# ScalarE's high copy of the first tile ahead of its copy of keys and queries, and two small changes in the tail, in a gated cross-attention and expert kernel

## What is computed

```python
# x (8,256,128), ctx (8,512,128), 16 heads of 64
xn   = layernorm(layernorm(x)) * gamma + beta
q, k, v = heads(xn @ w_q), *heads(split(ctx @ w_kv))
attn = softmax(q * 64**-0.5 @ k.T)
x    = x + tanh(g_xattn) * tanh(gate) * (merge(attn @ v) @ w_out + b_out)
# the expert layer's `combine` and `dispatch` follow from argmax and a cumulative count
p    = softmax(layernorm(x) @ gate_w)
slot = place of a token among those of its expert (dropped from 160 on)
y    = relu(expert_tokens @ w1[e]) @ w2[e]
out  = x + tanh(g_ffn) * p_max * y[slot]
```

## Time and profile before

| | |
|---|---|
| median of 3 runs | 475.69 us (475.61 to 476.74) |
| profiled execution | 475.53 us, of which the span of its instructions is 473.7 us |
| PE busy | 439.7 us, 93% |
| PEld busy | 334.0 us, 71% |
| ACT busy | 386.4 us, 82% |
| DVE busy | 360.3 us, 76% |
| POOL busy | 356.6 us, 75% |

### The profile page before, as it was taken

How to read it: one execution, slowest core, us unless ns; L and a number is a source line. 1 busy time by engine, 2 the same in 40 slices (tenths; PEclk the granted TensorE clock), 3 DMA queues, 4 the chain that set the end, 5 groups by cost and what they waited for, 6 DMA issues and landing times.

```text
span 473.7 us, 13155 instructions
## 1 busy us (share of the span) xinstructions
PE 439.7 (93%) x5096; PEld 334.0 (71%) x5096; DVE 360.3 (76%) x789; ACT 386.4 (82%) x630; POOL 356.6 (75%) x270
## 2 busy tenths in 40 slices
PE   7889799998999989999999999999999999988993
PEld 6656667776767767776777667776777677758892
DVE  4787687778877887779787796878877887785622
ACT  5889788899888988899888898899799998892330
POOL 3687686888788887888878877898878877871325
PEclk9999999999999999999999999999999999999998
DMA  5499999999999999999999999999989998996021
GB/s 167 150 177 192 206 187 175 170 181 204 188 176 188 210 194 180 192 192 192 198 189 197 189 196 191 185 200 209 190 157 185 193 180 147 159 182 137 14 67 46
DMA packets 283037, 82.10 MB, mean 173 GB/s; under 512 B 264387, under 2 KB 280435, under 8 KB 282976
## 3 DMA queue, kind: packets, MB, share of 16 engines
q1 hardware_dynamic: 281600, 77.96, 93.4%
q0 software_dynamic: 1376, 3.30, 2.2%
HBM read 10.83 MB, written 5.14 MB: 34 GB/s over the span
## 4 chain that ended last, share of the span: by engine, by line
PE 40%; DVE 20%; ACT 16%; DMA 10%; issue 8%; POOL 4%; POOLq 0%; SPq 0%; ACTq 0%; DVEq 0%
DVE MXL L903 9%; DMA PT<-PARTS 9%; ACT P L752 7%; DVE HL L890 4%; ACT HL L714 4%; PE psAB L1234 3%; PE psX L1319 3%; PE psAB L1241 3%; PE psO L1267 3%; ACT PARTS L762 3%; POOL PARTS L650 3%; PE psX L1355 3%; DVE VL L896 3%; PE psO L1269 3%; PE psO L1268 3%
## 5 line engine op out<-in xcount | busy, mean ns | idle before, releaser
L650 POOL TENSOR_TENSOR PARTS<-P,PARTS 128x1024 f16<-128x1024 f32 x125 | 267.4, 2145 | 63.5 <-ACT PARTS L762 61.8
L762 ACT ACTIVATE PARTS<-P 128x1024 f16<-128x1024 f32 x126 | 136.1, 1080 | 0.7
L752 ACT ACTIVATE P<-psAB,NB 128x512 f32<-128x512 f32 x128 | 81.6, 695 | 41.8 <-DVE NB L906 41.4
L903 DVE TENSOR_REDUCE MXL<-psAB 128x2 f32<-128x1024 f32 x64 | 78.4, 1224 | 41.4 <-PE psAB L1241 23.9
L1267 PE MATMUL psO<-VH,PT 128*128 128x65 f16 x1008 | 98.6, 194 | 8.3 <-DMA PT<-PARTS 7.7
L1267 PEld LDWEIGHTS psO<-VH,PT 128*128 128x128 f16 x1008 | 92.0, 98 | 12.0 <-DMA PT<-PARTS 8.9
L1268 PE MATMUL psO<-VL,PT 128*128 128x64 f16 x1008 | 98.5, 192 | 0.0
L1269 PE MATMUL psO<-VH,PT 128*128 128x65 f16 x1008 | 98.4, 193 | 0.0
L1268 PEld LDWEIGHTS psO<-VL,PT 128*128 128x128 f16 x1008 | 91.3, 98 | 0.5
L1269 PEld LDWEIGHTS psO<-VH,PT 128*128 128x128 f16 x1008 | 91.5, 97 | 0.0
L752 ACT ACTIVATE P<-psCD,NB 128x512 f32<-128x512 f32 x128 | 81.7, 703 | 0.1
(11 more groups left out here) (214 smaller groups left out, 871.7 us busy)
## 6 DMA issues: line engine op xcount, KB each, us to landing
ctx_raw<-in_ctx_dram SPq DMA_DIRECT2D x8, 256.0 KB, 3.7
w1s<-in_L_ffn_w_dram SPq DMA_DIRECT2D x8, 256.0 KB, 3.6
w2s<-in_L_ffn_w_dram SPq DMA_DIRECT2D x8, 256.0 KB, 4.0
PT<-PARTS SPq DMA_TRANSPOSE x126, 5.0
experts_table<-zeros POOLq DMA_DIRECT2D x2, 645.0 KB, 4.0
X<-in_x_dram SPq DMA_DIRECT2D x8, 128.0 KB, 4.2
wraw<-in_L_xattn_w_kv_dram SPq DMA_DIRECT2D x4, 256.0 KB, 5.3
out_dram<-row SPq DMA_DIRECT2D x8, 128.0 KB, 2.5
```

The source lines that it names most:

```text
L650: pool.tensor_tensor(PARTS[:, par, qt, 1], P32[:, par, qt], PARTS[:, par, qt, 0], ALU.subtract).then_inc(plo_done, 1)
L752: last = act.activation(P32[:, par, qt, SK * h:SK * h + SK], score_bank(qt)[:, SK * h:SK * h + SK], ACT.Exp, bias=NB[:, par, qt, h:h + 1])
L762: act.activation(PARTS[:, hp % 2, qt, 0], P32[:, hp % 2, qt], ACT.Copy).then_inc(phi_done[qt], 1)
L903: dve.tensor_reduce(MXL[:, par, qt, :, 0], score_bank(qt)[:].rearrange("p (h n) -> p h n", h=2), AX.X, ALU.max, negate=True).then_inc(max_ ...
```

## The change

In every step but the last, `phi(b, hp, 0)` moves from behind `kq_hi`, `v_hi` (hp 2), `xt_copy` (hp 4) and `tokt_copy` (hp 5) to a place right behind the exponentials of the first tile. In the tail, the values of pair 63 go to psAB instead of psO, with a third row of `rden`, and neither they nor the values of pair 62 wait for the division of the pair just ahead (63 waits for ScalarE to have read psAB, 62 for the division of 61). The output rows come in seven groups, (0,1) (2,3) (4) (5) (6) (7) (8,9), instead of five pairs; the last two groups stand behind the last `down`, and VectorE copies yT of the last two experts ahead of them.

```diff
@@ scalar engine, batch(b)
                     exps(b, hp, 0)
+                    if j < LAST:
+                        phi(b, hp, 0)
                     if not (is_last(b) and hp + AHEAD >= PAIRS):
                         kq_hi(*next_pair(b, hp, AHEAD))
...
                         tokt_copy(b - 1)
-                    if j < LAST:
-                        phi(b, hp, 0)
                     exps(b, hp, 1)
@@ values (tensor engine)
-                if j:
-                    pe.wait_ge(norm_done, turn(j) - 1)
+                sums = value_bank(j)
+                if j == LAST:
+                    pe.wait_ge(pthi_done, 1)
+                elif j:
+                    pe.wait_ge(norm_done, j)
...
-        OUT_GROUPS = ST_TILES // 2
-        ROWS_AFTER = [-(-2 * P * (i + 1) // CAP) - 1 for i in range(OUT_GROUPS)]
+        OUT_GROUPS = ((0, 1), (2, 3), (4,), (5,), (6,), (7,), (8, 9))
+        ROWS_AFTER = [-(-P * (tiles[-1] + 1) // CAP) - 1 for tiles in OUT_GROUPS]
...
+        def value_bank(j):
+
+            return psAB if j == LAST else psO
@@ after the experts (tensor engine)
             down(E - 1)
-            rows_out(OUT_GROUPS - 1)
+            for i, after in enumerate(ROWS_AFTER):
+                if after >= E - 2:
+                    rows_out(i)
```

More of the change, by code:

```diff
@@ L114, in gated_block @@
         NB = sb("NB", [P, 2, QT, 2], F32)
-        rden = sb("rden", [P, 2, 2 * QT], F32)
+        rden = sb("rden", [P, 3, 2 * QT], F32)
         O = sb("O", [P, QT, INNER], F32)
@@ L910, in normalise_heads @@
                 j = b * PAIRS + hp
-                sums = psO[:, 0:2 * QT * (DH + 1)].rearrange("p (g d) -> p g d", d=DH + 1)
+                sums = value_bank(j)[:, 0:2 * QT * (DH + 1)].rearrange("p (g d) -> p g d", d=DH + 1)
                 n = turn(j)
+                r = 2 if j == LAST else hp % 2
                 dve.wait_ge(pv_done, n)
-                dve.reciprocal(rden[:, hp % 2, :], sums[:, :, DH]).then_inc(rden_done, 1)
+                dve.reciprocal(rden[:, r, :], sums[:, :, DH]).then_inc(rden_done, 1)
                 dve.wait_ge(rden_done, n)
@@ L920, in normalise_heads @@
                 dve.tensor_tensor(o, sums[:, :, 0:DH].rearrange("p (h q) d -> p h q d", h=2),
-                                  rden[:, hp % 2, :].rearrange("p (h q) -> p h q", h=2).unsqueeze(3)
+                                  rden[:, r, :].rearrange("p (h q) -> p h q", h=2).unsqueeze(3)
                                   .to_broadcast([P, 2, QT, DH]), ALU.mult).then_inc(norm_done, 1)
@@ L1149, in y_rows @@
                 dve.wait_ge(yrow_psum, i + 1)
-                for n in range(2):
-                    t = 2 * i + n
+                for n, t in enumerate(OUT_GROUPS[i]):
                     dve.scalar_tensor_tensor(out=yrows[:, t, :], in0=FFN_BANKS[i % 2][:, P * n:P * n + P],
@@ L1158, in _ @@
                 dve.tensor_copy(yT[:, e * CAP:(e + 1) * CAP], [psO, psX][e % 2][:, 0:CAP]).then_inc(y_done, 1)
-                for i in range(OUT_GROUPS):
-                    if ROWS_AFTER[i] == e:
+                for i, after in enumerate(ROWS_AFTER):
+                    if after == e < E - 2 or after >= E - 2 and e == E - 1:
                         if i == 0:
@@ L1266, in values @@
                             first_, last_ = kt == 0, kt == KT - 1
-                            pe.matmul(psO[:, g:g + DH + 1], phi, VH[:, kt, head, 0:DH + 1], start=first_, stop=False)
-                            pe.matmul(psO[:, g:g + DH], phi, VL[:, kt, head, :], start=False, stop=False)
-                            last = pe.matmul(psO[:, g:g + DH + 1], plo, VH[:, kt, head, 0:DH + 1], start=False,
+                            pe.matmul(sums[:, g:g + DH + 1], phi, VH[:, kt, head, 0:DH + 1], start=first_, stop=False)
+                            pe.matmul(sums[:, g:g + DH], phi, VL[:, kt, head, :], start=False, stop=False)
+                            last = pe.matmul(sums[:, g:g + DH + 1], plo, VH[:, kt, head, 0:DH + 1], start=False,
                                              stop=last_)
@@ L1480, in rows_out @@
                 if i >= 2:
[L1482 to L1485, removed]
+                    pe.wait_ge(final_done, OUT_GROUPS[i - 2][-1] + 1)
+                for n, t in enumerate(OUT_GROUPS[i]):
+                    last = pe.transpose(FFN_BANKS[i % 2][:, P * n:P * n + P], yT[:, P * t:P * t + P], ident[:])
                 last.then_inc(yrow_psum, 1)
@@ L1517, in _ @@
                     spread(e + 2)
[L1518 to L1522, removed]
+                for i, after in enumerate(ROWS_AFTER):
+                    if after == e - 2:
                         rows_out(i)
             down(E - 1)
-            rows_out(OUT_GROUPS - 1)
+            for i, after in enumerate(ROWS_AFTER):
+                if after >= E - 2:
+                    rows_out(i)
 _INS = ['x', 'ctx_1024', 'g_xattn', 'g_ffn', 'L0_xattn_ln_gamma', 'L0_xattn_ln_beta', 'L0_xattn_w_q',
```

## The result

| | before | after |
|---|---|---|
| median | 475.69 us (475.34 to 476.74, 5 runs) | 495.75 us (495.36 to 495.88, 5 runs) |
| profiled execution, its span | 475.53, 473.7 us | 495.81, 493.8 us |

The ratio is 1.0399, with a 95% interval of 1.0361 to 1.0436: the kernel is slower by 4.0%. The forecast was 496.2 us.

The account below looks back on a forecast made before the run. The prediction took TensorE's stream, busy 93% of the span, as the bound. Late readers cost 23.5 us, less 2.0 for transposed parts, 0.5 and 0.3 in the tail: +20.7 on 475.5, so 496.2 us, range 484 to 501.

Parts of the forecast that it names:

- hp 2, six batches: At hp 2 the context transposes wait for a later `v_lo`, without slack: 1.11 us in six batches, 6.7 us.
- hp 4 and hp 5: Late `xt_copy` delays the value projection at hp 4, 5.2 us; the late token copy delays one at hp 5, 1.5.
- hp 3: At hp 3 a late `add_attention` delays the projection beyond its slack in seven batches: 3.8 us.
- hp 1: At hp 1 the delay exceeds the slack ahead of the projection in seven batches: 3.2 us.
- hp 7 into hp 0: Late `kq_lo` and `v_lo` on VectorE delay the ranks at hp 0, batches 2 to 7: 3.1 us.
- transposed parts: TensorE's waits for transposed parts shrink because first tiles' parts come earlier: -2.0 us, about half of 4.3.
- tail: In the tail pair 62's values lose their wait, -0.5 us, and the scatters of output rows theirs, -0.3 us.
- The delay: On ScalarE `kq_hi`, `v_hi` and `xt_copy` start 1.11 us later, behind the moved high copy.
- (a): Rival: earlier parts remove every wait for transposed parts, the tail gives 0.8 us: 467.0 us; chance 0.08.
- (b): Rival: only places without slack cost, so each batch pays at hp 2 and 4 alone: 484.6 us; chance 0.14.
- (c): Rival: TensorE has room and absorbs late readers, so only the tail shows: 474.7 us; chance 0.04.
- The signs: Trace of after: about 1.8 us idle at hp 2, 1 at hp 4, new waits at hp 1, 3, 0, none in tail.

Follow-up runs that it names:

- hp 2 alone: The kernel before with the first tile's high copy (`phi`) moved up in the steps of hp 2 only; 481.80 us, ratio 1.0126.
- hp 4 alone: The kernel before with the first tile's high copy (`phi`) moved up in the steps of hp 4 only; 476.43 us, ratio 1.0004.
- half dose: The kernel after with the first tile's high copy split in two halves, the second left in the old place; 483.45 us, ratio 1.0166.
- hp 1, 3 and 7 alone: The kernel before with the first tile's high copy moved up at hp 1, 3 and 7 only; 484.01 us, ratio 1.0163.
- the tail alone: The kernel after with the high copy back in its old place, so only the tail's changes; 474.48 us, ratio 0.9972.
- ScalarE's order alone: The kernel before with the first tile's high copy moved and nothing of the tail; 498.42 us, ratio 1.0467.
- the first and the third kernel on psX: The first: the kernel after with readers of psX, then `phi`, then `kq_hi`, and `v_lo` ahead of `kq_lo`; 483.96 us, ratio 1.0156.
- the third kernel on psX: The kernel before with the changed tail, and at hp 4 alone the order `xt_copy`, `phi`, `kq_hi`; 474.34 us, ratio 0.9955.

## Why the prediction was right, point by point

| term | predicted | measured, lengths of steps |
|---|---|---|
| hp 2, six batches | 6.7 | 6.5 |
| hp 4 and hp 5 | 5.2 + 1.5 | 6.5 - 1.1 |
| hp 3 | 3.8 | 4.4, and 1.5 of a lower clock |
| hp 1 | 3.2 | 3.5 |
| hp 7 into hp 0 | 3.1 | 4.3 |
| batch 0 | 0 | -0.2 |
| transposed parts | -2.0 | -4.1 |
| tail | -0.8 | -1.0 |
| start of the program | 0 | -0.3 |

**The delay and the two places without slack.** 1.11 us predicted, 1.12 read at `kq_hi`, 1.08 paid by each of twelve steps. Here the prediction held in mechanism and in size, and the runs with hp 2 and hp 4 alone show that the cost belongs to these places.

**hp 4 with hp 5.** The cost at hp 4 was right, what comes back at hp 5 was not: I took 0.24 us from the wait that was printed, and alone it gives back 0.55. In the kernel after it is 0.2 net, and the token copy (tT) now has TensorE waiting in its turn, 0.19 us printed. The two were sized 1.3 us too high together.

**The places with slack.** The half dose shows the rule that the prediction used, delay less slack, with the slacks read from the distances in the earlier trace rows: 0.51 measured at hp 3 (0.55 read), 0.62 at hp 1 in five batches (0.65 read there, more in the one of the earlier trace rows), 0.33 at hp 0 (0.28 read). The one place read wrong is hp 3 in batch 7, 0.97 us instead of 0.4: with hp 2 alone it pays 0.14, with hp 3 and not hp 2 0.07, with both 0.97. In that batch the step of hp 2 got no longer in any of these kernels; that TensorE therefore meets at hp 3 a ScalarE that is late twice is my reading, which no run isolates.

**The transposed parts, the term that was mis-sized.** I took half of the 4.3 us, on the ground that the second tiles' parts move with the late ScalarE. That holds for a delay well ahead of them (hp 2 alone, and hp 1, 3 and 7 alone: the wait of batch 1 stayed), but not for the one at hp 4: there the transfers were issued 0.15 and 0.27 us later for a TensorE that came 0.86 us later. In the kernel after all four waits behind the 4.3 us are gone, so the whole bound was won (one of the four lies in batch 0 and is counted in its row). 0.9 of the 4.1 us is the wait of batch 4 that only the profile of the kernel before has at that place; with the tail alone hp 7 of that batch is 1.0 us longer in its stead, so how much of it the change took is open. Yet 1.2 us of that was paid back at once at hp 0: those waits at hp 7 had been the cover of hp 0 in batches 2 and 3, for which I had put 0.3 us each or nothing; with those waits left in place (hp 1, 3 and 7 alone) hp 0 cost nothing there, and with the waits gone 0.9 and 1.0. The two terms are one: predicted +1.1 together, measured +0.2.

**The rivals.** (a) fell: the waits for parts did shrink, by 4.1 us against 24 that the places cost, and at hp 7 because TensorE came later, not because parts came earlier. (b) fell with the run of hp 1, 3 and 7 alone, 484.01 us where it says no change. (c) fell: TensorE is busy for 90% and its weight loads for 68%, and yet a delay of 1.12 us on ScalarE came through as 1.08 at twelve places. The Trainium skill (Perfetto Trace Analysis, Identifying the Most-Contended Engine) would have judged the room of TensorE by its share of peak arithmetic or the share of its weight loads; here the share of weight loads said nothing of whether late readers could be absorbed, and the distances from release to start said it place by place.

**What the prediction had not seen.** Two steps of hp 3 cost 0.73 us more than their sisters because of TensorE's clock (below), 1.5 us. That the sum is only 0.6 us off is partly luck, misses of both signs: 2.1 us less for the transfers and 1.3 less at hp 4 and 5, against 1.2 more at hp 0 and 2.1 more at hp 3.

**The signs.** TensorE's wait at hp 2 (1.8 us said, 1.74 read) and at hp 4 (1 and 1.06) came as written, those at hp 1, hp 3 and of the ranks smaller (0.16, 0.38 and 0.44 us printed, where 0.3 to 0.6 and 0.8 were said), probably because modelled ends hide part. ScalarE's idle time ahead of the first exponentials did not grow in step 34 (1.92 us in both), whose scores come ahead of TensorE's wait at hp 2; it did in the next step, from 0.45 to 1.39 us. Over the span it is 41.4 us in the kernel before, and 49.4 + 3.8 after:

```profile
ACT P L752 <- DVE NB L906: 41.4, 41, 2.2
```

```profile
ACT P L757 <- DVE NB L911: 49.4, 49, 2.2
...
ACT P L757 <- POOL PARTS L655: 3.8, 2, 1.9
```

Nearly all of the growth of ScalarE's idle time stands there: that went from 473.7 - 386.4 = 87.3 to 493.8 - 394.5 = 99.3 us, 12.0, and TensorE's from 34.0 to 49.8, 15.8. What is left of the 20.1 us is ScalarE's busy time, 8.1 us more for the same 630 instructions: the second exponentials come 0.15 us later in a step, which the prediction named, because a copy that reads the result of the exponentials no longer overlaps them. GpSimd waits longer for high copies, 83.3 us against 61.8, without harm.

**The tail.** The wait of 0.48 us before pair 62's values is gone, no row of TensorE between the values of 61 and the end of those of 62 has idle time printed, and the scatters of tiles 2 to 9 run without a gap. Those of tiles 5 and 6, beside the earlier trace rows:

```profile
485.07 0.97 POOL L683 DMA_INDIRECT out_dram<-P,target  x1 [0.30 <-issue]
...
486.34 0.97 POOL L683 DMA_INDIRECT out_dram<-P,target  x1 [0.30 <-issue]
```

Together it gave 1.0 us in the profiled execution, where 0.8 was said, but one execution can't settle a microsecond there: from the transposes of the last exponentials on, five executions with the old tail took 48.6 to 50.6 us and six with the new one 47.6 to 49.9. That the signs came is shown; that the tail gained is not.

## What to carry to other kernels

On an engine that works in order, a copy that is moved up costs each reader behind it its whole length (here 0.96 us, and 0.15 for an overlap that is lost), less the slack of that place; read the slack as the distance from the release to the start of the waiting product, also where no idle time is printed, and sum place by place. Where a change makes the bounding engine late, look for waits on a chain that doesn't move with it: they shrink by nearly as much (here 0.75 of 0.86 us), and what they covered behind them comes up in turn. If one wait of 0.66 us repeats in every batch, see first if the engine whose copies the readers wait for has a gap there; here ScalarE had only one of 0.35 us, and another order moved the wait to the next reader.

## What the runs showed that I had not expected

**TensorE's clock falls after some of the new waits, not after all.** Three stretches of the kernel after in batch 1: around the wait of 1.74 us at hp 2, right behind it, and later (the columns: stretch, its us, busy time of PE, PEld, DVE, ACT and POOL, the granted clock, share and rate of DMA):

```profile
84.00:87.00 3.00, 1.26 (x26) 1.00 (x24) 2.07 (x4) 3.00 (x6) 2.09 (x1) 1.00 1.05 114
87.40:90.80 3.40, 3.40 (x14) 2.19 (x13) 2.60 (x4) 1.72 (x4) 3.27 (x3) 0.50 0.79 151
91.00:94.00 3.00, 3.00 (x50) 2.99 (x49) 1.77 (x4) 3.00 (x5) 2.17 (x2) 1.00 1.01 195
```

A granted clock of 0.50 is the level of 1.2 GHz, 1.00 that of 2.4 GHz. TensorE had been busy for 1.26 of the 3.00 us ahead of the fall. The same happened in batch 5, and the two steps of hp 3 behind took 8.58 and 8.59 us instead of 7.84. The other four waits of the same length were followed by no such fall; with ScalarE's order alone it came once, in batch 6, and with hp 2 alone, which has the same six waits, not at all. Such a fall also stands at hp 4 of batch 0 with hp 4 alone and with hp 1, 3 and 7 alone, and in the tail of the first and the third kernel on psX; these tails are 0.7 and 1.3 us longer than that of the kernel before. What decides when it comes stays open.

**The release behind a row of products can come one to two microseconds late.** In the kernel of the half dose, TensorE's last `down` has its rows end as in the kernel after, but VectorE's copy of its result starts late. The row of that copy in the kernel of the half dose:

```profile
473.26 0.33 DVE L1172 COPY VH<-psX 128x160 f32<-128x160 f32 x1 [2.34 <-remote]
```

and in the kernel after:

```profile
485.88 0.33 DVE L1163 COPY VH<-psX 128x160 f32<-128x160 f32 x1 [0.51 <-PE psX L1509]
```

The word "remote" says that the profile found nothing on this core that released it. On that the scatters of the last three tiles waited, and the tail became 2 us longer. The same copy is late in two more of the six executions with the new tail, by 1.1 us (idle time of 1.66 us with the tail alone and 1.60 in the third kernel on psX, where the kernel after has 0.51). With the tail alone:

```profile
464.45 0.32 DVE L1163 COPY VH<-psX 128x160 f32<-128x160 f32 x1 [1.66 <-PE psX L1509]
```

So the tail alone shows little of its gain in its profile. A late release stands in the old tail too, with ScalarE's order alone, at the division of pair 61:

```profile
452.18 0.18 DVE L914 RECIPROCAL rden<-psO 128x4 f32<-128x4 f32 x1 [1.12 <-remote]
...
453.09 0.20 PE L1267 MATMUL psO<-VH,wraw 128*128 128x65 f16 x1 [1.16 <-DVE O L920]
```

There the values of pair 63 wait 1.16 us for it; in the new tail they no longer wait for that division. In the half dose the granted clock was 1.00 around the late release, so a lower clock is not the cause; what the cause is was not found. With hp 2 alone the same wait is 1.17 us, and the same old tail took 49.9 us in that execution and 48.6 in that of the kernel before.
